# A perceiver's second cross attention on one core: softmax sums added on GpSimd, gathered rows projected tile by tile

## The reference

```python
    def _L1_xattn_ref(q, kv, Wq, Wkv, Wc):
        qp = jnp.einsum('bld,ed->ble', q, Wq)
        scores = jnp.einsum('bld,bmd->blm', qp, kv)
        idx = jnp.argmax(scores, axis=-1)
        mem = jnp.take_along_axis(kv, idx[..., None], axis=1)
        mkv = jnp.einsum('bld,ed->ble', mem, Wkv)
        mk, mv = jnp.split(mkv, 2, axis=-1)
        qh = qp.reshape(b, l, h, dh).transpose(0, 2, 1, 3)
        logits = jnp.einsum('bhld,bmd->bhlm', qh, mk) * scale
        attn = jax.nn.softmax(logits, axis=-1)
        out = jnp.einsum('bhlm,bmd->bhld', attn, mv)
        ...
        return jnp.einsum('bld,ed->ble', out, Wc)
```

## Time and profile before

| | us |
|---|---|
| median of three runs | 1172.11 |
| the three runs | 1169.98, 1175.34, 1172.11 |
| the profiled execution | 1167.67 |
| its span | 1165.9 |
| TensorE busy over the span | 1033.3 (89%) |
| VectorE, ScalarE, GpSimd busy | 872.5, 489.4, 325.8 |

### The profile page before, as it was taken

The page is one execution under the profiler, slowest core; times in us unless marked ns, Lnnn a source line. Parts: engine busy times, 40 slices in busy tenths (PEclk is TensorE's granted clock), DMA queues, the critical chain, the costliest instruction groups (busy, mean ns, idle before and its releaser), DMA issues.

```text
span 1165.9 us, 14433 instructions
## 1 busy us (share of the span) xinstructions
PE 1033.3 (89%) x4820; PEld 486.2 (42%) x4820; DVE 872.5 (75%) x1199; ACT 489.4 (42%) x733; POOL 325.8 (28%) x165
## 2 busy tenths in 40 slices
PE   7999999699999989699277999999898889886796
PEld 3444444244444435344133444444622144464353
DVE  5599999799999266777853499999377349474796
ACT  2354554566666547047751201100044524345163
POOL 4245554100000833000020577775100020281003
PEclk9999999799999999799688999999979989997898
DMA  6145555433433536120012154454100200000000
GB/s 241 61 128 189 176 171 179 164 108 127 154 117 106 193 140 238 43 91 1 0 73 82 67 201 185 166 196 113 36 1 1 74 2 1 1 1 1 2 1 36
DMA packets 41827, 112.60 MB, mean 97 GB/s; under 512 B 4512, under 2 KB 15296, under 8 KB 35648
## 3 DMA queue, kind: packets, MB, share of 16 engines
q1 hardware_dynamic: 38592, 101.13, 24.8%
q10 hardware_dynamic: 2880, 9.96, 2.6%
...
...
## 4 chain that ended last, share of the span: by engine, by line
PE 62%; DVE 14%; issue 3%; ACT 3%; POOL 0%; DVEq 0%; ACTq 0%; POOLq 0%
PE PS L793 5%; PE PS L794 5%; PE PS L795 5%; PE PS L1603 5%; PE PS L1605 5%; PE PS L1604 5%; PE PS L249 4%; PE PS L251 4%; PE PS L250 4%; PE PS L1671 3%; DVE arena L1894 2%; PE PS L1649 1%; PE PS L1588 1%; PE PS L1694 1%; PE PS L2178 1%
## 5 line engine op out<-in xcount | busy, mean ns | idle before, releaser
L793 PE MATMUL PS<-arena 128*128 128x512 f16 x256 | 98.3, 384 | 3.6 <-DVE arena L673 3.6
L763 PE MATMUL PS<-arena 128*128 128x512 f16 x256 | 97.2, 380 | 2.1 <-DVE arena L606 2.0
L1603 PE MATMUL PS<-arena 128*128 128x512 f16 x256 | 97.1, 379 | 1.8 <-DVE arena L1488 1.8
L794 PE MATMUL PS<-arena 128*128 128x512 f16 x256 | 98.4, 384 | 0.0
L795 PE MATMUL PS<-arena 128*128 128x512 f16 x256 | 98.2, 384 | 0.0
L764 PE MATMUL PS<-arena 128*128 128x512 f16 x256 | 97.2, 380 | 0.0
L1605 PE MATMUL PS<-arena 128*128 128x512 f16 x256 | 97.1, 379 | 0.0
L765 PE MATMUL PS<-arena 128*128 128x512 f16 x256 | 97.1, 379 | 0.0
L1604 PE MATMUL PS<-arena 128*128 128x512 f16 x256 | 97.1, 379 | 0.0
L479 POOL TENSOR_TENSOR arena<-arena 128x2048 f16<-128x2048 f32 x16 | 66.0, 4126 | 33.5 <-ACT arena L530 33.1
L249 PE MATMUL PS<-arena 128*128 128x512 f16 x112 | 45.0, 402 | 33.9 <-DVE arena L1252 28.5
...
## 6 DMA issues: line engine op xcount, KB each, us to landing
...
```

What stands on the lines that cost most here:

```text
L763: pe.matmul(bank, CHI[:, b, e, cols], QHI[:, e, :], start=(e == 0), stop=False)
L793: pe.matmul(PS[:, t, :], PHI[:, j, cols], CHI[:, b, j, :], start=False, stop=False)
L794: pe.matmul(PS[:, t, :], PHI[:, j, cols], CLO[:, b, j, :], start=False, stop=False)
L1603: pe.matmul(bank, QHI3[:, e, cols], CHI3[:, b, e, :], start=(e == 0), stop=False)
```

## The change

1. *Denominators.* `weigh(b)` multiplies by the values alone, at `n % 4 == 1`. GpSimd adds the exponentials of a group over the tiles `m` = 0 to 3, head by head, in f32, into `ACC[g % 2]` (4 x 512; the room of `WQ1`, which is no longer needed, and `XT`): 12 additions a group, the first of each head reading two slots of `PT`. In the last group the fourth tile isn't added, so there are 8, and 44 in all. `sums(g)` then multiplies `ACC` by ones into bank 7, four matmuls, once a group: after the entry at `n % 16 == 4` of the next group, and at the end for the last one, where four matmuls over the last four slots of `PT` are added. It waits for GpSimd by `s3_acc`. ScalarE waits before it writes a slot again for `s3_acc` too, and `weighted(g)` waits for `sums(g)`.
2. *Gathered rows.* Each gather has its own semaphore. Tile `t` is turned by four transposes into bank `t`, copied by ScalarE into the columns of that tile, and projected to keys by four products of 128 columns; the products of tile t - 1 stand behind the turn of tile t. The values of tiles 0 and 1 come ahead of the first entry, those of tiles 2 and 3 behind the entries 1 and 2; VectorE copies them at entry 4 instead of 2.
3. *Semaphores.* `ln_stats` and `ln_rstd` become one count, `s3_clip` and `s3_whole` become one count, and the sigmoid's own semaphore gives way to ScalarE's general one. Each wait still asks for the same instruction. These pieces of the diff are left out below.

```diff
@@ -1319,6 +1317,7 @@
         PT = view(106 * K, [16, N])
         ATTT = view(138 * K, [DT, N])
         DEN = view(154 * K, [N])
+        ACC = [view(86 * K, [4, N]), XT]
 
         WINH = view(0, [4 * DT, QP], F16)
         WINL = view(18 * K + 512, [4 * DT, QP], F16)
...
@@ -1348,7 +1346,8 @@
         s3_scores = sem("s3_scores")
         s3_max = sem("s3_max")
         s3_idx = sem("s3_idx")
-        s3_mem = sem("s3_mem")
+        s3_mem = [sem(f"s3_mem{t}") for t in range(NT)]
+        s3_acc = sem("s3_acc")
         s3_memt_psum = sem("s3_memt_psum")
         s3_memt = sem("s3_memt")
         s3_kv_psum = sem("s3_kv_psum")
...
@@ -1404,6 +1403,11 @@
             e = FIRST + 9 * (n // 16) + STEPS.index(n % 16)
             return e if e < ENTRIES else None
 
+        def added(n):
+
+            g, m, j = n // 16, (n // 4) % 4, n % 4
+            return 12 * g + 4 * max(m - 1, 0) + j + 1
+
         def shift_entry(g):
 
             return g * (PAIRS_G + 1) + PAIRS_G
...
@@ -1437,8 +1441,22 @@
             for t in range(NT):
                 pool.indirect_dma_start(out=MEM[:, t, :], out_offset=None, in_=a["ctx"],
                                         in_offset=bass.IndirectOffsetOnAxis(ap=MEMIDX[:, t:t + 1], axis=0)
-                                        ).then_inc(s3_mem, 16)
+                                        ).then_inc(s3_mem[t], 16)
             pool.memset(MKS[96:98, :], MSHIFT).then_inc(pool_marks, 1)
+            for n in range(UNITS):
+                g, m, j = n // 16, (n // 4) % 4, n % 4
+                if m == 0 or n >= UNITS - 4:
+                    continue
+                acc = ACC[g % 2][:, j, :]
+                pool.wait_ge(s3_p, n + 1)
+                if m == 1:
+                    if j == 0 and g >= 2:
+                        pool.wait_ge(pe_marks, PE_MARK[f"s3_sums{g - 2}"])
+                    left = PT[:, (n - 4) % 16, :]
+                else:
+                    pool.wait_ge(s3_acc, added(n - 4))
+                    left = acc
+                pool.tensor_tensor(acc, left, PT[:, n % 16, :], ALU.add).then_inc(s3_acc, 1)
 
         def s3_act(act, link):
             transpose_x_act(act, 3)
...
@@ -1458,9 +1476,10 @@
             for r, part in enumerate((QHI3, QLO3, QHI3)):
                 for j in range(4):
                     act.dma_start(stacked[r * DH:(r + 1) * DH, j], part[j * DH:(j + 1) * DH, :, :]).then_inc(s3_qst, 16)
-            for c in range(DT):
-                act.wait_ge(s3_memt_psum, c + 1)
-                act.copy(MEMT[:, c, :], PS[:, c, :]).then_inc(s3_memt, 1)
+            for t in range(NT):
+                act.wait_ge(s3_memt_psum, t + 1)
+                cols = slice(t * P, (t + 1) * P)
+                act.copy(MEMT[:, :, cols], PS[:, t, :].rearrange("p (c l) -> p c l", c=DT)).then_inc(s3_memt, 1)
 
             act.wait_ge(s3_kv_psum, 1)
             act.activation(MKS[0:96, :], PS[0:96, 4, :], ACT.Copy, scale=float(DH) ** -0.5).then_inc(act_marks, 1)
...
@@ -1477,6 +1496,7 @@
                 act.wait_ge(s3_logits, n + 1)
                 if n >= 16:
                     act.wait_ge(s3_pv, n // 4 - 3)
+                    act.wait_ge(s3_acc, added(n - 16))
                 act.activation(PT[:, n % 16, :], PS[:, 4 + n % 2, :], ACT.Exp).then_inc(s3_p, 1)
                 if n % 16 == 10 and n // 16 < GROUPS - 1:
                     shift_hi(n // 16 + 1)
...
@@ -1542,6 +1562,7 @@
             def weighted(g):
 
                 dve.wait_ge(s3_pv, 4 * g + 4)
+                dve.wait_ge(pe_marks, PE_MARK[f"s3_sums{g}"])
                 if g < GROUPS - 1:
                     dve.tensor_copy(DEN, PS[:, 7, :]).then_inc(s3_den, 1)
                     dve.tensor_copy(ATTT[:, g, :], PS[:, 6, :]).then_inc(s3_den, 1)
...
@@ -1562,7 +1583,7 @@
                     shift_lo(g)
                 else:
                     take_max(e)
-                if e == 2:
+                if e == 4:
                     dve.wait_ge(s3_kv_psum, 2)
                     dve.tensor_copy(MVAL, PS[:, 7, 0:NT * DH].rearrange("p (a b) -> p a b", a=NT)).then_inc(s3_kv, 1)
 
...
@@ -1607,15 +1628,38 @@
                         ins.then_inc(s3_scores, 1)
             pe.wait_ge(s3_idx, MT + AHEAD_BANK)
             keep_warm(pe, 7, 6)
-            pe.wait_ge(s3_mem, 16 * NT)
-            for c in range(DT):
-                for t in range(NT):
-                    ins = pe.transpose(PS[:, c, t * P:(t + 1) * P], MEM[:, t, c * P:(c + 1) * P], IDENT[:, :])
+
+            def turn_mem(t):
+
+                pe.wait_ge(s3_mem[t], 16)
+                for c in range(DT):
+                    ins = pe.transpose(PS[:, t, c * P:(c + 1) * P], MEM[:, t, c * P:(c + 1) * P], IDENT[:, :])
                 ins.then_inc(s3_memt_psum, 1)
-            pe.wait_ge(s3_memt, DT)
-            for c in range(DT):
-                ins = pe.matmul(PS[:, 4, :], WK1[:, c, :], MEMT[:, c, :], start=(c == 0), stop=(c == DT - 1))
-            ins.then_inc(s3_kv_psum, 1)
+
+            def keys(t):
+
+                cols = slice(t * P, (t + 1) * P)
+                pe.wait_ge(s3_memt, t + 1)
+                for c in range(DT):
+                    ins = pe.matmul(PS[:, 4, cols], WK1[:, c, :], MEMT[:, c, cols], start=(c == 0), stop=(c == DT - 1))
+                if t == NT - 1:
+                    ins.then_inc(s3_kv_psum, 1)
+
+            def values(t):
+
+                for c in range(DT):
+                    ins = pe.matmul(PS[:, 7, t * DH:(t + 1) * DH], MEMT[:, c, t * P:(t + 1) * P], WV1[:, c, 0:DH],
+                                    start=(c == 0), stop=(c == DT - 1))
+                if t == NT - 1:
+                    ins.then_inc(s3_kv_psum, 1)
+
+            turn_mem(0)
+            for t in range(1, NT):
+                turn_mem(t)
+                keys(t - 1)
+            keys(NT - 1)
+            values(0)
+            values(1)
             pe.wait_ge(s3_kv, 1)
             pe.wait_ge(s3_qst, 12 * 16)
             pe.wait_ge(pool_marks, POOL_MARK["s3_ones"])
...
@@ -1649,45 +1693,49 @@
                 pe.matmul(PS[:, 4 + n % 2, :], MKS[0:98, m * P:(m + 1) * P], QST[0:98, 4 * g + j, :],
                           start=True, stop=True).then_inc(s3_logits, 1)
 
-            def values():
-
-                for t in range(NT):
-                    for c in range(DT):
-                        ins = pe.matmul(PS[:, 7, t * DH:(t + 1) * DH], MEMT[:, c, t * P:(t + 1) * P], WV1[:, c, 0:DH],
-                                        start=(c == 0), stop=(c == DT - 1))
-                ins.then_inc(s3_kv_psum, 1)
-
-            def weigh(b, bank):
+            def weigh(b):
 
                 g, m = b // 4, b % 4
-                if bank == 6:
-                    pe.wait_ge(s3_p, 4 * b + 4)
-                    if b == 0:
-                        pe.wait_ge(s3_kv, 2)
+                pe.wait_ge(s3_p, 4 * b + 4)
+                if b == 0:
+                    pe.wait_ge(s3_kv, 2)
                 if m == 0 and g:
-                    pe.wait_ge(s3_den, 3 * (g - 1) + (2 if bank == 6 else 1))
+                    pe.wait_ge(s3_den, 3 * (g - 1) + 2)
                 for j in range(4):
-                    left = MVAL[:, m, :] if bank == 6 else ONES[:, 0:DH]
-                    ins = pe.matmul(PS[DH * j:DH * (j + 1), bank, :], left, PT[:, (4 * b + j) % 16, :],
+                    ins = pe.matmul(PS[DH * j:DH * (j + 1), 6, :], MVAL[:, m, :], PT[:, (4 * b + j) % 16, :],
                                     start=(m == 0), stop=(m == NT - 1))
-                if bank == 7:
-                    ins.then_inc(s3_pv, 1)
+                ins.then_inc(s3_pv, 1)
+
+            def sums(g):
+
+                last = g == GROUPS - 1
+                pe.wait_ge(s3_acc, added(16 * g + (11 if last else 15)))
+                if g:
+                    pe.wait_ge(s3_den, 3 * (g - 1) + 1)
+                for j in range(4):
+                    ins = pe.matmul(PS[DH * j:DH * (j + 1), 7, :], ONES[:, 0:DH], ACC[g % 2][:, j, :],
+                                    start=True, stop=not last)
+                if last:
+                    for j in range(4):
+                        ins = pe.matmul(PS[DH * j:DH * (j + 1), 7, :], ONES[:, 0:DH], PT[:, 12 + j, :],
+                                        start=False, stop=True)
+                ins.then_inc(pe_marks, 1)
 
             for e in range(FIRST):
                 entry(e)
-                if e == 1:
-                    values()
-            for n in range(UNITS + LAG):
+                if e in (1, 2):
+                    values(e + 1)
+            for n in range(UNITS + 6):
                 if n < UNITS:
                     shifted(n)
                     e = entry_at(n)
                     if e is not None:
                         entry(e)
-                if n >= LAG and n % 4 == 3:
-                    weigh((n - LAG) // 4, 6)
-                if n >= LAG + 5 and n % 4 == 1:
-                    weigh((n - LAG - 2) // 4, 7)
```

(6 more changed lines are left out.)

29 lines of the change are left out of this document (13 added, 16 removed).

## The result

| | before | after |
|---|---|---|
| median, timed together (20 runs each), us | 1175.2 | 1168.67 |
| ratio after to before, 95% interval | | 0.995 (0.9935 to 0.9966) |
| profiled execution, us | 1167.67 | 1169.17 |
| its span; mean granted clock | 1165.9; 0.941 | 1167.4; 0.939 |
| TensorE busy over the span, us | 1033.3 | 1028.5 |

A forecast was written before the change was run, and what follows sets the result against it. It took TensorE, with its `weigh` calls, as the bound in the steady pattern, though not everywhere. Gain 6.4 - 0.4 (adds) - 1.0 (locks) - 0.7 (clock) = 4.3 us, set against the three-run median: 1167.8 us, range 1163.0 to 1173.5.

The forecast's parts named there:

- The case forecast: Whole kernel: gain of 3 to 5.8 us, taken as 4.3, chance 0.42.
- 1.2 - 0.4: At `weighted(0)`: gain 1.2 us, less 0.4 because `sums(0)` waits for GpSimd's add 15.
- 2.2 - 0.4 - 0.5: Low half of shift 2: gain 2.2 us, less 0.4 for GpSimd's adds and 0.5 for the product waiting half an add.
- 6.4 - 0.4 - 1.0 - 0.7: Last reciprocal: gain 6.4 us, less 0.4 for GpSimd's adds, 1.0 for two products' waits, 0.7 for the low clock.
- Gathered rows: Stage start: tile-by-tile rows and split values bring group 0's units 0.8 us earlier, 0.2 at entry 0 and 0.6 after.
- The division and the wait for it: `weighted` takes 5.4 us, making VectorE the late one at shift 2; unit 48 newly waits for SyncE's transfer, about 2.4 us.
- From unit 48 to the last reciprocal: Last units, ScalarE the bound: 14.8 us instead of 16.1, with `sums(3)` waiting 0 for GpSimd's eight adds.
- Locks: VectorE's product in `weighted(0)` and `weighted(1)` waits half a GpSimd add each, 1.0 us together; the reciprocal is not hit.
- The clock: Before unit 48 TensorE does little; a low clock there costs some 1.4 us, half counted, 0.7.
- Rival 2: TensorE's three waits, before unit 28, at 898 and before unit 48, each bring the low clock: gain 0 to 2 us, chance 0.17.
- nothing changes: From the end of the last `weighted` to the end of the kernel: no further gain or loss.
- Rivals 1 and 3: 1: nothing eats the gain of 6.4 us, chance 0.30; 3: GpSimd becomes the bound, 1180 us, chance 0.11.

The follow-up runs named there:

- e2: Kernel before with only the gathered rows tile by tile, values split and semaphores merged; denominators by TensorE as before: ratio to before 0.9967.
- e3: Changed kernel with each GpSimd add on 32 of the 512 columns, other columns left out: ratio to before 0.9927.
- e1: Changed kernel with the gathered rows handled as before, so only the changed sums and merged semaphores: ratio to before 0.9988.
- e8: Changed kernel with eight GpSimd adds in every group (32, not 44), TensorE summing the fourth tile: ratio to before 0.9985.
- e10: Changed kernel with two dummy products on TensorE behind each of the entries 3 to 12: ratio to before 0.9937.
- e4: Changed kernel with 16 dummy products on TensorE behind the last sums, ahead of the projection: ratio to before 0.9913.
- e5: e1 with dummy products in two TensorE stalls, ten behind unit 28 and seven before unit 48: ratio to before 0.998.
- e12: Kernel before with the divisions of groups 0 to 2 behind the last shift row and 16 dummy products ahead of the projection: ratio 0.9977.

## Why the prediction was right, and where its steps were off

The case forecast came about: a gain of 3 to 5.8 us, measured 5.9 (4.0 to 7.6), and in the trace 4.64 at the last reciprocal against 4.3. The size is in part luck. Up to unit 48 the gain was 1.9 us larger than forecast, behind it 1.6 us smaller, and where the clock falls moved other traces of this stage by 2 to 4 us. The 1167.8 too is nearer to the 1168.67 than its parts: it starts from a median of three runs, 1172.11, where twenty gave 1175.2, and the gain was larger than forecast. Step by step, gains against before from the first dummy product:

| point | forecast | measured |
|---|---|---|
| first entry | 0.2 | 0.28 |
| unit 0 | 0.8 | 2.70 |
| low half of shift 1 | 1.0 | 2.21 |
| `weighted(0)` | 1.2 - 0.4 | 1.84 |
| low half of shift 2 | 2.2 - 0.4 - 0.5 | 2.38 |
| `weighted(1)` | 2.4 - 0.4 - 0.5 | 2.65 |
| unit 48 | 5.1 - 0.4 - 1.0 | 5.60 |
| last reciprocal | 6.4 - 0.4 - 1.0 - 0.7 | 4.64 |
| end of the span | the same | 3.52 |

- **Gathered rows.** The term was mis-sized, 0.8 for 2.70, mostly by the step that turned VectorE's 2.14 us into 0.4 + 1.1: the values of a later tile take 0.98 us, and nothing of that pause was left. With the 0.28 of the first entry that is 2.42 of the 2.70. And the low clock among the entries set in a little later (granted 0.82 in the 4 us from +24, 0.50 there before). The 2.70 us weren't kept: 0.5 went by low 1, 0.4 more by `weighted(0)`, where the sum had expected to gain, and alone (e2) this part gave 0.21 at the end in the trace, 0.33% in time.
- **The division and the wait for it.** Right in kind at both places: VectorE became the late one at shift 2, and unit 48 waits for the row's transfer, 1.91 us, the new wait that was forecast.
- **From unit 48 to the last reciprocal.** 14.8 + 0.7 forecast, 17.05 measured (910.22 to 927.27), nearly 1 us more than before. This is the step that failed, by 1.6 us. I had `sums(3)` wait 0 because eight adds of 1.2 us from 909.0 end in time. But an add is 1.27 us, and GpSimd came to the end of group 2 late (after, seven adds without a pause):

```profile
904.72 9.07 POOL L1459 TENSOR_TENSOR arena<-arena 128x512 f32<-128x512 f32 x7
```

  `sums(2)` waited 0.61 for the last of them and, with the exponentials behind it late, `sums(3)` 0.63 for the last add of all. From low 3 to the last reciprocal it is 19.48 us in after and 17.95 with narrow adds (e3). The price of an add was taken from 128x580 (1.14 scaled); the 1.27 lies inside the range of 1.0 to 2.0, but each tenth of a us more than was taken counts 12 times a group.
- **Locks.** I put 0.5 us on each of two products; they took 1.12 instead of 0.69, 0.43 each, and 1.76 once, off the path. It is a wait in line, as the starts show (after, single rows; the first product is the one at 888.26 shown above):

```profile
888.79 1.71 POOL L1459 TENSOR_TENSOR XT<-XT,arena 128x512 f32<-128x512 f32 x1
```
```profile
921.00 1.76 DVE L1572 TENSOR_TENSOR arena<-arena 128x512 f32<-128x512 f32 x1
```
```profile
922.17 1.73 POOL L1459 TENSOR_TENSOR XT<-XT,arena 128x512 f32<-128x512 f32 x1
```

  The product at 888.26 began 0.53 us before the next add and took 0.43 longer; the one at 921.00 began 1.17 before the next, and took 1.07 longer. Each waited for the running add but for 0.10 us, and the next add took 0.45 longer in its turn. The reciprocals beside adds took 3.35 us as before. The Trainium skill, SBUF — State Buffer, section Who interferes with whom, has this: two SBUF inputs on VectorE and a GpSimd instruction that reads SBUF exclude each other, one input doesn't. This case's rows agree, by the 1.12 and 1.76 us of the product and the 3.35 of the reciprocal.
- **The clock.** Half a low stretch, 0.7, was counted before unit 48. It didn't come in this trace (clock 1.00 from 910.2 to 916.2). Rival 2 named the right danger, though: of the kernels that share this stop, e1, e8 and e10 had the low clock behind it, and after, e4 and e3 (1.49 us there) not. From the last reciprocal to the end after takes 240.13 us and before 239.01; "nothing changes" was wrong by 1.1, of which 0.85 is the projection's start at the low clock (9.68 against 8.83 us).
- **Rivals 1 and 3.** GpSimd didn't become the bound of the whole (1.27, not 1.45 us an add), so 3 was wrong; that nothing eats (1) was wrong too.

What stays open: by the traces the gain at the end is 3.5 us, by the runs 5.9. Before was profiled in one of its quickest executions, whose low stretch among the entries ended at +40.2 where that of e1, e5 and e12 ended at +43.6, and e1, e5 and e12, which share its order of the gathered rows, reach unit 0 at +37.86, +38.00 and +38.26, not +37.63, while all kernels with the new order but e10 reach it at +34.9 to +35.0. That fits a gain somewhat larger than the pair of traces shows; how much of the rest lies in where the clock falls in the later stages wasn't measured.
